# A four-branch graph network: degree reciprocals spread by DMA instead of by matmuls, zero stores issued in two row stages, and each chunk's mean taken ahead of the edge shares

## The chip, the cores and the metric

One core of a Trainium2 chip runs the program. The metric is the device time of one execution in microseconds (us), here the median of three. Engine names are those of the profile: PE (TensorE; PEld is its weight load), DVE (VectorE), ACT (ScalarE), POOL (GpSimd), SP (SyncE, which here only issues DMAs).

## The reference

The graph has 6250 nodes of 128 features and 106,250 edges, sorted by destination. Four blocks follow each other, each with a residual and a layernorm over a node's features:

```
x = layernorm(x + L0(x))   # three rounds: (h + sum of h[src] over edges into dst) @ W1, batchnorm, relu, @ W2
x = layernorm(x + L1(x))   # row, col = src, dst: agg = segment_sum(x[col], row) / max(deg, 1); relu(agg @ W1.T + b1) @ W2.T + b2
x = layernorm(x + L2(x))   # agg = segment_sum(x[src], dst) / max(deg, 1); h = agg @ W_l.T + b_l + x @ W_r.T; batchnorm, relu, + x
x = layernorm(x + L3(x))   # edge-weighted segment max, then edge-weighted mean, weights normalised per destination
```

Two vectors of degrees matter here: `deg` over the sources for L1 and `deg` over the destinations for L2. Their reciprocals scale whole columns of a `[features, nodes]` array, so every one of the 128 partitions needs the same 6250 numbers.

## The kernel before

The nodes are cut into 10 chunks (`NBLK`) of 625 columns (`BLK`), each of five tiles of 125 (`TN`). A message sum is done as a dense product: a matrix of edge counts stands in DRAM (`counts`, and transposed in `turned`), in panels of 0.8 MB, ten panels (`NSUB`) to a chunk. SP loads the panels into four buffers (`PAN`), and PE multiplies each with the node rows, which are split into three bf16 parts (`XP`, `HH`): 30 matmuls to a panel (line 524), 300 to a chunk. `pe_dense` runs such a pass; passes 1 and 2 serve L0, pass 3 (with `scales=True`) serves L1 and reads `turned`, pass 4 serves L2. Between passes lie the batchnorms and "row stages", in which PE, ACT and DVE pass single chunks back and forth (`act_unit_rows` before pass 3, `act_mean_rows` before pass 4). The row steps of a stage are woven into the first chunk of the next pass (`steps_between`): six steps stand before its first panel, one before each further one.

Where the order comes from: each engine's list is written out by hand, and engines meet only at counting semaphores. An engine works strictly through its own list, and so does a DMA queue's issuer: a DMA that ACT issues stands between ACT's other instructions.

What the change touches:

- **The reciprocals.** DVE computes them as 125 partitions x 50 (`rin` for L2, in `dve_in_degrees`; `rdeg` for L1, in `dve_row_sums`). To bring 625 of them onto all partitions DVE lays five of the 50 columns out as diagonal matrices (lines 994 and 1052), PE multiplies a matrix of ones with them (lines 507 and 514), and ACT copies the product out of PSUM into `DEG` (line 588) or `A` (line 1403). That happens once a chunk, ten times in pass 1 and ten times in pass 3.
- **The edge shares.** 104 groups of edges are handled beside passes 1 and 3, 52 in each (`WEIGH_AT`: seven or six groups to a chunk in pass 1, six in pass 3). For a group ACT issues two loads of 0.576 MB (`share_loads`, line 578; two buffers), DVE compares and sums them (`dve_shares`, line 845), and POOL scatters the result into the array `shares` in DRAM (line 761).
- **The zeros.** `shares` has to be zero before the scatters reach it. Half is zeroed at the start. The rest takes 25 stores of 3.2 MB from a zero array in DRAM (`blank_slices`, line 565): five after pass 1, one a chunk in pass 2, and ten together at the start of `act_unit_rows`.
- **The mean in pass 3.** `dve_mean` takes chunk c's six groups of shares first and then multiplies chunk c's sums with its reciprocals (line 1062). PE's linear layer of that chunk (line 488) needs this product. It stands before panel 3 of chunk c + 1.

Of the kernel before, what the change touches and what calls it, by code (L numbers as in the profile page):

```python
# [41 lines left out]
ZEROS_AT = {"dense1": (0,) * 10, "taken1": 5, "dense2": (1,) * 10, "taken2": 10}  # L42
# [5 lines left out]
def build_program(nc, a, out):  # L48
# [3 lines left out]
    with ctx:  # L52
# [14 lines left out]
        blank = nc.dram_tensor("blank", [128, 6400], F32).ap()  # L67
        share_rows = nc.dram_tensor("share_rows", [1, EP + 256], F32).ap()
# [114 lines left out]
        in_mat = [AA[0:TN, 5000 + b * BLK:5000 + (b + 1) * BLK].rearrange("p (j n) -> p j n", n=TN) for b in range(2)]  # L183
# [4 lines left out]
        scale_mat = [SS[b][0:TN, :].rearrange("p (j n) -> p j n", n=TN) for b in range(2)]  # L188
# [25 lines left out]
        degree_ps = [PS[:, 2048 + 512 * h:2048 + 512 * h + n] for h, n in ((0, HALF), (1, BLK - HALF))]  # L214
# [48 lines left out]
        in_diag = sem("in_diag")  # L263
        in_full = sem("in_full")
        in_kept = sem("in_kept")
        scale_diag = sem("scale_diag")
        scale_full = sem("scale_full")
        scale_kept = sem("scale_kept")
# [209 lines left out]
        def pe_dense(pe, n, lin, terms, ready, taken=None, degrees=False, scales=False, own=True, between=None):  # L478
# [13 lines left out]
            for c in range(NBLK):  # L492
# [5 lines left out]
                for s in range(NSUB):  # L498
# [3 lines left out]
                    if degrees and s == (1 if c else NSUB - 1):  # L502
                        pe.wait_ge(in_diag, c + 1)
                        pe.wait_ge(in_kept, c + 2)
                        for h, (lo, w) in enumerate(((0, HALF), (HALF, BLK - HALF))):
                            last = nc.tensor.matmul(degree_ps[h], ones[0:TN, :],
                                                    AA[0:TN, 5000 + b * BLK + lo:5000 + b * BLK + lo + w],
                                                    start=True, stop=True)
                        last.then_inc(in_full, 1)
                    if scales and s == (1 if c else NSUB - 1):  # L510
                        pe.wait_ge(scale_diag, c + 1)
                        pe.wait_ge(scale_kept, c + 2)
                        for h, (lo, w) in enumerate(((0, HALF), (HALF, BLK - HALF))):
                            last = nc.tensor.matmul(degree_ps[h], ones[0:TN, :], SS[b][0:TN, lo:lo + w],
                                                    start=True, stop=True)
                        last.then_inc(scale_full, 1)
# [67 lines left out]
        def keep_degrees(act, c):  # L584

            act.wait_ge(in_full, c + 1)
            for h, (lo, w) in enumerate(((0, HALF), (HALF, BLK - HALF))):
                last = nc.scalar.activation(DEG[:, c * BLK + lo:c * BLK + lo + w], degree_ps[h], ACT.Copy)
            last.then_inc(in_kept, 1)

        def act_dense(act, n):

            for c in range(NBLK):
                if n == 1:
                    keep_degrees(act, c)
# [3 lines left out]
                if n == 1 and c == 0:  # L599
                    act.wait_ge(xp_ready, 2 * NBLK)  # L600
# [389 lines left out]
        def dve_in_degrees(dve):  # L990

            def spread(c):
# [10 lines left out]
            dve.drain()  # L1003
            nc.vector.reciprocal(rin[0:TN, :], rin[0:TN, :])
            dve.drain()
            spread(0)
            spread(1)
            dve_unit_weights(dve)
            dve.wait_ge(unit_rows, 1)
# [1586 lines left out]
```

## Time and profile before

| | us |
|---|---|
| median of three runs | 4531.61 (4524.09 to 4542.86) |
| profiled execution, its own time | 4542.64 |
| span of its profile | 4540.8 |
| granted TensorE clock, mean of the span | 0.930 |

The span falls into the build of the matrices with pass 0 (to about 1240 us), pass 1 (1277 to 1736), pass 2 (1774 to 2225), the first row stage and pass 3 (2232 to 2764), the second row stage and pass 4 (2765 to 3229), the row stage of L2 (to 3300) and L3 (to the end). Durations below are from this one execution, so sums are made against its own time. A view with 40 digits cuts its window in 40 equal slices; a digit is the busy share in tenths.

### The profile page before, as it was taken

What the parts mean: (1) busy time and instruction counts of PE and PEld (TensorE: products, weight loads), DVE (VectorE), ACT (ScalarE), POOL (GpSimd) and SP (SyncE); (2) the same over time, 40 slices, a digit from 0 to 9 for tenths busy, and PEclk for the clock granted to TensorE, in tenths of its full rate; (3) what the DMA queues carried; (4) which work ended last, traced back from release to release, by engine and by line L of the source; (5) the groups of instructions that cost most, each with busy time, mean ns of one, the idle gap of its engine ahead of it and who ended that gap; (6) DMA issues with size and microseconds to landing.
All of it is one profiled execution on the core that took longest, in us unless ns stands there. A gap on an engine that the chain in (4) does not pass through costs nothing.

```text
span 4540.8 us, 71772 instructions
## 1 busy us (share of the span) xinstructions
PE 3528.8 (78%) x24919; PEld 2671.7 (59%) x24919; DVE 2066.2 (46%) x5903; ACT 1059.9 (23%) x2743; POOL 2450.1 (54%) x2510
## 2 busy tenths in 40 slices
PE   0005987555589998899769998999847898989898
PEld 0004766444466665677546776777546777777776
DVE  6543434443254556877655544000333444444445
ACT  0003655333420002000130003000323333333331
POOL 4777777777203444444305443444267777777750
PEclk9999998777799999999889999999868999999999
DMA  9999999887449998788899993666244777767665
GB/s 373 368 363 360 368 368 336 291 282 266 165 151 334 351 360 279 262 282 278 282 341 331 360 340 123 189 196 195 86 128 159 243 261 246 259 236 261 237 232 188
DMA packets 307375, 1218.26 MB, mean 268 GB/s; under 512 B 86273, under 2 KB 98850, under 8 KB 290811
## 3 DMA queue, kind: packets, MB, share of 16 engines
q1 hardware_dynamic: 143706, 705.58, 43.9%
q10 hardware_dynamic: 83489, 453.14, 27.0%
q0 software_dynamic: 79872, 55.32, 5.2%
q8 instruction: 207, 3.39, 0.3%
q14 instruction: 101, 0.83, 0.1%
HBM read 958.19 MB, written 337.54 MB: 285 GB/s over the span
## 4 chain that ended last, share of the span: by engine, by line
PE 42%; POOL 23%; DMA 16%; issue 10%; DVE 4%; ACT 2%; POOLq 1%; ACTq 1%; DVEq 0%; SPq 0%
PE PS L524 30%; POOL PAN L389 18%; DMA counts<-SSB 8%; POOL counts L735 5%; PE PS L446 4%; DMA BB<-share_rows 4%; DMA counts<-val_slot,idx_slot 2%; PE PS L1462 2%; PE PS L452 1%; DMA PAN<-counts 1%; PE PS L488 1%; DVE ST L845 1%; DMA PAN<-turned 1%; DVE X L882 1%; PE PS L1112 1%
## 5 line engine op out<-in xcount | busy, mean ns | idle before, releaser
L761 POOL DMA_INDIRECT shares<-dst_f,spare x832 | 810.2, 974 | 1247.6 <-DMA shares<-dst_f,spare 468.7
L524 PE MATMUL PS<-PAN,HH 125*128 125x375 bf16 x8000 | 1413.3, 299 | 36.8 <-DMA PAN<-turned 12.1
L389 POOL DMA_INDIRECT PAN<-table,src_i x832 | 820.0, 986 | 347.8 <-issue 273.1
L735 POOL DMA_INDIRECT counts<-val_slot,idx_slot x832 | 807.1, 970 | 350.0 <-issue 323.0
L524 PEld LDWEIGHTS PS<-PAN,HH 125*128 125x128 bf16 x8000 | 780.8, 98 | 340.2 <-issue 34.0
L524 PE MATMUL PS<-PAN,XP 125*128 125x375 bf16 (+1 forms) x4000 | 866.3, 298 | 0.0
L446 PE MATMUL PS<-PAN,HH 125*128 125x375 bf16 x2000 | 363.7, 305 | 608.9 <-DMA PAN<-counts 608.9
L446 PEld LDWEIGHTS PS<-PAN,HH 125*128 125x128 bf16 x2000 | 180.4, 101 | 650.6 <-issue 485.4
L524 PEld LDWEIGHTS PS<-PAN,XP 125*128 125x128 bf16 x4000 | 390.5, 98 | 153.0 <-issue 3.7
L656 ACT ACTIVATE X<-PS 125x625 bf16<-125x625 bf16 x500 | 345.2, 692 | 453.2 <-PE PS L452 441.6
L882 DVE TENSOR_REDUCE X<-PAN 125x5 f32<-125x3125 bf16 x100 | 334.2, 3399 | 76.0 <-DMA PAN<-counts 76.0
L1548 ACT ACTIVATE BB<-PAN,ew 128x128 f32<-128x128 f32 x832 | 254.2, 388 | 476.4 <-DMA PAN<-table,src_i 476.4
L845 DVE SCALAR_TENSOR_TENSOR BB<-BB 128x255 bf16<-128x255 f32 x312 | 135.3, 485 | 392.4 <-DMA BB<-share_rows 392.1
L1462 PE MATMUL PS<-XP,HH 125*128 125x375 f32 (+1 forms) x1000 | 287.3, 436 | 13.0 <-DVE HH L1654 13.0
L1462 PE MATMUL PS<-PAN,HH 125*128 125x375 f32 (+1 forms) x1000 | 288.3, 437 | 1.8 <-issue 1.8
L907 DVE SCALAR_TENSOR_TENSOR ST<-BB,spare 128x255 bf16<-128x255 f32 x624 | 262.5, 484 | 35.7 <-DMA BB<-key_rows 18.3
L928 DVE CAST val_slot<-acc 128x8 bf16<-128x8 f32 x104 | 21.9, 211 | 562.1 <-DMA counts<-val_slot,idx_slot 561.7
L1614 DVE TENSOR_TENSOR_SCAN BB<-BB,PS 128x1024 f32<-128x1024 f32 x104 | 243.4, 2340 | 15.3 <-PE PS L1430 15.3
L452 PEld LDWEIGHTS PS<-ident_h,PAN 125*125 125x125 bf16 x2500 | 213.8, 141 | 51.2 <-ACT X L656 19.2
L452 PE MATMUL PS<-ident_h,PAN 125*125 125x125 bf16 x2500 | 230.7, 224 | 11.5 <-ACT X L656 11.3
L1641 DVE TENSOR_TENSOR DEG<-DEG,PS 128x375 f32<-128x375 f32 (+1 forms) x180 | 85.7, 480 | 330.8 <-PE PS L1462 330.8
L1462 PEld LDWEIGHTS PS<-XP,HH 125*128 125x128 f32 x1000 | 187.1, 195 | 77.7 <-DVE HH L1654 14.7
(271 smaller groups left out, 3937.7 us busy)
## 6 DMA issues: line engine op xcount, KB each, us to landing
PAN<-counts SPq DMA_DIRECT2D x300, 800.0 KB
counts<-SSB ACTq DMA_DIRECT2D x10, 8000.0 KB, 35.8
shares<-SSB SPq DMA_DIRECT2D x50, 1600.0 KB
PAN<-counts ACTq DMA_DIRECT2D x100, 800.0 KB
shares<-blank ACTq DMA_DIRECT2D x25, 3200.0 KB, 22.9
XP<-shares SPq DMA_DIRECT2D x50, 1600.0 KB
PAN<-shares SPq DMA_DIRECT2D x50, 1600.0 KB
turned<-X ACTq DMA_DIRECT2D x100, 781.2 KB
```

Of the source, the lines that this page charges most:

```text
L389: nc.gpsimd.indirect_dma_start(out=gbuf[g % 2][:, k, :], out_offset=None, in_=source, in_offset=bass.IndirectOffsetOnAxis(ap=src_i[:, t:t ...
L446: nc.tensor.matmul(dense_ps[b][h], xpart[part][0:TN, s * SUBJ + j, :], panel[u % NPAN][0:TN, j, lo:lo + w], start=(s == 0 and j == 0 and p ...
L452: last = nc.tensor.transpose(turn_ps[m][0:TN, k, 0:TN], panel[u % NPAN][0:TN, k, j * TN:(j + 1) * TN], ident_h[0:TN, 0:TN])
L524: last = nc.tensor.matmul(dense_ps[b][h], xpart[part][0:TN, s * SUBJ + j, :], (turned_tile if scales else panel)[u % NPAN][0:TN, j, lo:lo ...
L656: nc.scalar.activation(stage[u % NTURN][0:TN, t, :, :], turn_ps[m][0:TN, :, 0:TN], ACT.Copy, accum_out=in_sums[:, s, bass.ds(i * (2 * TPB) ...
L735: nc.gpsimd.indirect_dma_start(out=counts_flat, out_offset=bass.IndirectOffsetOnAxis(ap=idx_slot[b][:, k:k + 1], axis=0), in_=val_slot[b][ ...
L761: nc.gpsimd.indirect_dma_start(out=shares_flat, out_offset=bass.IndirectOffsetOnAxis(ap=share_at[:, t:t + 1], axis=0), in_=share[:, t:t + ...
L882: nc.vector.tensor_reduce(out=sums[:, c, p * SUBJ:(p + 1) * SUBJ], in_=panel[u % NPAN][0:TN, :, 0:BLK], axis=AX.X, op=ALU.add).then_inc(pa ...
L907: last = nc.vector.scalar_tensor_tensor(out=junk[k], in0=KR[b][:, k * 128:k * 128 + NEAR], scalar=key_e[:, at(k, 1)], in1=mask[:, :], op0= ...
L1462: last = nc.tensor.matmul(part_ps[h], h_rows[0:TN, c * SUBJ + j, :], wpanel[u % NWP][0:TN, j, lo:lo + w], start=(j == 0), stop=(j == SUBJ ...
L1548: last = nc.scalar.activation(weighed[:, k, :], gbuf[g % 2][:, k, :], ACT.Copy, scale=ew[:, g * GT + k:g * GT + k + 1])
L1614: nc.vector.tensor_tensor_scan(scan[g % 2], pen[g % 2], msg_ps, scan[1 - g % 2][:, GE - 1:GE], ALU.add, ALU.max).then_inc(scanned, 1)
```

## The change

The reciprocals go through a small DRAM array, `degree_rows`. `store_degrees` writes the 125 x 50 array into it in the order of the nodes (`(j p) -> p j`, so that neighbours in a partition lie 500 bytes apart in DRAM, and every 4-byte number is a run by itself). `spread_degrees` reads the row of 6250 numbers back onto all 128 partitions (a 3.2 MB load). Both are issued by ACT. The diagonals, the matmuls with ones and the copies out of PSUM are gone. The ten zero stores at the start of `act_unit_rows` are gone from there; one now follows each of five steps of that row stage and of the next. In `dve_mean` a chunk's product stands before its shares, and in `act_scales` four of a chunk's six share loads stand behind the next linear output.

```diff
-        def keep_degrees(act, c):
-            act.wait_ge(in_full, c + 1)
-            for h, (lo, w) in enumerate(((0, HALF), (HALF, BLK - HALF))):
-                last = nc.scalar.activation(DEG[:, c * BLK + lo:c * BLK + lo + w], degree_ps[h], ACT.Copy)
-            last.then_inc(in_kept, 1)
+        def store_degrees(act, which, rows, ready, out_sem):
+            act.wait_ge(ready, 1)
+            act.dma_start(degree_rows[which:which + 1, :].rearrange("o (j p) -> p (o j)", p=TN), rows[0:TN, :],
+                          allow_slow_non_contiguous=True
+                          ).then_inc(out_sem, 16)
+        def spread_degrees(act, which, to, out_sem, spread_sem):
+            row = degree_rows[which:which + 1, :]
+            act.wait_ge(out_sem, 16)
+            act.dma_start(to, bass.AP(row.tensor, row.offset, [[0, 128], [1, N]])).then_inc(spread_sem, 16)
...
         def act_dense(act, n):
             for c in range(NBLK):
-                if n == 1:
-                    keep_degrees(act, c)
                 if c:
                     act_linear_chunk(act, 2 * n, c - 1, ACT.Identity, f"L0_b1_{n}", A)
                 keep_dense(act, n, c // 2, c % 2)
                 if n == 1 and c == 0:
+                    store_degrees(act, 0, rin, rin_ready, rin_out)
...
                 if n == 1:
                     if c == 1:
                         act.wait_ge(share_rows_out, 16 * 3)
+                    if c == 3:
+                        spread_degrees(act, 0, DEG[:, 0:N], rin_out, rin_spread)
                     share_loads(act, WEIGH_AT[1][c])
...
         def dve_mean(dve):
-            scale(0, 0)
-            scale(0, 1)
             dve.wait_ge(xp_ready, 4 * NBLK)
             share_keys(dve)
             for c in range(NBLK):
+                if c == 0:
+                    dve.wait_ge(rdeg_spread, 16)
+                mean(c // 2, c % 2)
                 dve_shares(dve, WEIGH_AT[3][c])
-                mean(c // 2, c % 2)
-                if c + 2 < NBLK:
-                    scale(c // 2 + 1, c % 2)
...
             act.wait_ge(bn_coef, 5)                      # act_unit_rows
             for c in range(2):
                 act_affine_chunk(act, A, c)
-            blank_slices(act, ZEROS_AT["taken2"], known=False)
+            store_degrees(act, 1, rdeg, rdeg_ready, rdeg_out)
             for k in range(NBLK + 3):
...
+                blank_slices(act, int(1 < k < 7), known=False)
...
         def act_mean_rows(act):
...
+                blank_slices(act, int(k < 7), known=False)
...
         def act_scales(act):
+            spread_degrees(act, 1, A[:, 0:N], rdeg_out, rdeg_spread)
             act.wait_ge(xp_ready, 4 * NBLK)
             for c in range(NBLK):
-                act.wait_ge(scale_full, c + 1)
-                for h, (lo, w) in enumerate(((0, HALF), (HALF, BLK - HALF))):
-                    last = nc.scalar.activation(A[:, c * BLK + lo:c * BLK + lo + w], degree_ps[h], ACT.Copy)
-                last.then_inc(scale_kept, 1)
                 if c == 3:
                     blank_slices(act, 0)
-                share_loads(act, WEIGH_AT[3][c] // 2)
                 if c:
                     act_linear_chunk(act, 6, c - 1, ACT.Relu, "L1_b1", A)
-                share_loads(act, WEIGH_AT[3][c] - WEIGH_AT[3][c] // 2)
+                    share_loads(act, WEIGH_AT[3][c - 1] - min(WEIGH_AT[3][c - 1], 2))
+                share_loads(act, min(WEIGH_AT[3][c], 2))
```

`pe_dense` loses the two blocks that issued the matmuls with ones. `act_linear_chunk` of pass 4 now confirms the last zeros to POOL at chunk 3. Both arrays of reciprocals are stored and spread once.

How the lists read, first ACT's at the start of the first row stage. L1223 (L1192 after) is the affine step, L565 (L548) a zero store, L570 the new store of reciprocals. Before:

```order
606 L1894 ACTIVATE cf<-mv,eps_bn 128x1
607 L1223 ACTIVATE AA<-AA,cf 128x625 x2
608 L565 DMA shares<-blank 128x6400 x10
609 L1223 ACTIVATE AA<-AA,cf 128x625 x2
610 L1231 ACTIVATE SSB,col_slot<-PS 125x128 x5
```

The same place after the change:

```order
588 L1862 ACTIVATE cf<-mv,eps_bn 128x1
589 L1192 ACTIVATE AA<-AA,cf 128x625 x2
590 L570 DMA degree_rows<-rdeg 125x50x1
591 L1192 ACTIVATE AA<-AA,cf 128x625 x2
592 L1200 ACTIVATE SSB,col_slot<-PS 125x128 x5
...
598 L1178 ACTIVATE ST<-ST,row_mv,row_sd 125x128 x5
599 L1183 ACTIVATE HH<-ST 125x640
600 L548 DMA shares<-blank 128x6400
601 L1192 ACTIVATE AA<-AA,cf 128x625
```

One store of 125 x 50 single numbers has taken the place of ten zero stores, and the first zero store has moved behind the first normalized chunk.

DVE's list at the start of pass 3, where L845 (L835 after) are the shares and L1062 (L1032) is the mean. Before:

```order
733 L1052 TENSOR_TENSOR SSB<-ident,rdeg 125x625 x2
734 L833 SCALAR_TENSOR_TENSOR BB<-keyloc,src_i 128x832
735 L845 SCALAR_TENSOR_TENSOR BB,dst_f<-BB 128x255 x3
736 L845 SCALAR_TENSOR_TENSOR ST,dst_f<-BB 128x255 x5
...
746 L845 SCALAR_TENSOR_TENSOR ST,dst_f<-BB 128x255 x5
747 L1062 TENSOR_TENSOR AA<-AA,PS 128x375
748 L1062 TENSOR_TENSOR AA<-AA,PS 128x250
749 L1052 TENSOR_TENSOR SSB<-ident,rdeg 125x625
```

After:

```order
724 L823 SCALAR_TENSOR_TENSOR BB<-keyloc,src_i 128x832
725 L1032 TENSOR_TENSOR AA<-AA,PS 128x375
726 L1032 TENSOR_TENSOR AA<-AA,PS 128x250
727 L835 SCALAR_TENSOR_TENSOR BB,dst_f<-BB 128x255 x3
728 L835 SCALAR_TENSOR_TENSOR ST,dst_f<-BB 128x255 x5
```

The mean of chunk 0 has moved ahead of the first six groups, and the diagonals (L1052) are gone.

ACT's list where pass 3 begins. L1403 is the copy out of PSUM, L578 (L561 after) a share load, L546 (L529) the output of the linear layer, L578 after the change the spread. Before:

```order
675 L1219 ACTIVATE X<-PS 128x625
676 L1403 ACTIVATE AA<-PS 128x375
677 L1403 ACTIVATE AA<-PS 128x250
678 L578 DMA BB<-key_rows 128x1151
679 L578 DMA BB<-share_rows 128x1151
```

After:

```order
662 L1188 ACTIVATE X<-PS 128x625
663 L578 DMA AA<-degree_rows 128x6250
664 L561 DMA BB<-key_rows 128x1151
665 L561 DMA BB<-share_rows 128x1151
666 L561 DMA BB<-key_rows 128x1151
667 L561 DMA BB<-share_rows 128x1151
668 L529 ACTIVATE AA<-PS,vectors 128x625
669 L561 DMA BB<-key_rows 128x1151
```

The first linear output now stands behind two groups' loads, where nine stood ahead of it before.

## Rows read from the trace of the kernel before

**Rows 1.** Busy by stretch: PE, PEld, DVE, ACT, POOL, PEclk, DMA share, GB/s. Pass 1.
```profile
1371.00:1420.00 49.00, 47.23 (x353) 33.87 (x351) 22.59 (x109) 2.89 (x7) 17.69 (x19) 1.00 1.00 373
```
**Rows 2.** The same view, the two row stages.
```profile
2225.00:2345.00 120.00, 75.17 (x390) 50.41 (x391) 67.98 (x240) 61.65 (x203) 0.00 (x0) 0.77 1.00 351
2764.00:2835.00 71.00, 58.00 (x356) 40.94 (x357) 44.80 (x159) 34.81 (x81) 16.69 (x17) 0.95 0.27 83
```
**Rows 3.** Timeline of ACT, passes 1 and 2: start, us, instruction [idle before <-releaser].
```profile
1327.68 0.48 ACT L552 ACTIVATE AA<-PS 128x375 f32<-128x375 f32 x1 [4.10 <-PE PS L473]
1370.96 0.48 ACT L552 ACTIVATE AA<-PS 128x375 f32<-128x375 f32 x1 [26.23 <-PE PS L473]
...
1735.98 0.75 ACT L552 ACTIVATE AA<-PS 128x375 f32<-128x375 f32 x2 [17.40 <-PE PS L473]
...
2182.22 0.48 ACT L552 ACTIVATE AA<-PS 128x375 f32<-128x375 f32 x1 [28.28 <-PE PS L473]
2224.45 0.48 ACT L552 ACTIVATE AA<-PS 128x375 f32<-128x375 f32 x1 [28.28 <-PE PS L473]
```
**Rows 4.** Waits of PE from 1270 to 1740 us: total, times, longest.
```profile
PE PS L506 <- DVE AA L994: 11.6, 4, 3.9
```
**Rows 5.** DMA from 1371 to 1736 us: all; one queue (packets, MB, share).
```profile
DMA packets 32000, 127.37 MB, mean 349 GB/s; under 512 B 8416, under 2 KB 8416, under 8 KB 31968
...
q0 software_dynamic: 5472, 0.10, 1.1%
```
**Rows 6.** Timeline of ACT, start of the first row stage.
```profile
2231.37 17.67 ACTq L565 DMA_DIRECT2D shares<-blank  x8
2249.09 1.71 ACT L1223 ACTIVATE AA<-AA,cf 128x625 f32<-128x625 f32 x2 [17.20 <-issue]
...
2259.59 0.74 ACT L1214 ACTIVATE HH<-ST 125x640 bf16<-125x640 f32 x1
```
**Rows 7.** Chain that ended last, 2215 to 2400 us: start, us, what.
```profile
2276.10 4.18 PE PS L524 x30
...
2309.67 33.81 DMA PAN<-turned
...
2349.90 1.07 PE PS L514 x4
```
**Rows 8.** Line 524 of PE, whole span: idle before it until, us, times.
```profile
  DMA PAN<-turned: 12.1, 3
```
**Rows 9.** Timeline of PE, first linear layer of pass 3.
```profile
2392.40 2.47 PE L488 MATMUL PS<-AA,weights 128*128 128x512 f32 x4 [24.25 <-DVE AA L1062]
```
**Rows 10.** Chain that ended last, second row stage.
```profile
2791.49 4.03 PE PS L524 x30
...
2834.93 24.20 PE PS L524 x180
2859.13 2.15 PE PS L488 x8
```
**Rows 11.** Chain that ended last, inside pass 3.
```profile
2480.28 32.27 PE PS L524 x240
...
2522.75 32.27 PE PS L524 x240
```
**Rows 12.** DMA issues: KB each, median us from issue to landing.
```profile
BB<-in_x_rows ACTq DMA_DIRECT2D x1, 3200.0 KB, 24.9
```
**Rows 13.** Line 1741: SP issues ten stores of 125 partitions, duration ns min/median/max.
```profile
L1741 SPq DMA_DIRECT2D out<-BB x10: 264/2712/5948, 4499.9 to 4534.5; - x10
```
**Rows 14.** DMA from 4503 to 4541 us: share in 40 slices; the queue.
```profile
DMA  9923433333333333333333343333333100233300
...
q1 hardware_dynamic: 6380, 4.02, 34.2%
```
**Rows 15.** Timeline of POOL in pass 2, two scatters of 128 numbers.
```profile
2203.09 0.96 POOL L761 DMA_INDIRECT shares<-dst_f,spare  x1 [0.30 <-issue]
2204.35 0.95 POOL L761 DMA_INDIRECT shares<-dst_f,spare  x1 [0.30 <-issue]
```

More of the change, by code:

```diff
@@ L182, in build_program @@
         in_sums = DEG[0:TN, 5728:5728 + NBLK * NBLK * TPB].rearrange("p (c j) -> p c j", c=NBLK)
-        in_mat = [AA[0:TN, 5000 + b * BLK:5000 + (b + 1) * BLK].rearrange("p (j n) -> p j n", n=TN) for b in range(2)]
         near_w, near_k, same, before, behind = (BB[0:G, j * KRW:(j + 1) * KRW] for j in range(5))
@@ L187, in build_program @@
         sums = X[0:TN, 0:NBLK * NBLK * TPB].rearrange("p (c j) -> p c j", c=NBLK)
-        scale_mat = [SS[b][0:TN, :].rearrange("p (j n) -> p j n", n=TN) for b in range(2)]
         KR = [BB[:, b * KRW:b * KRW + KRS] for b in range(2)]
@@ L262, in build_program @@
         turned_out = [sem(f"turned_out{u}") for u in range(NTURN)]
[L263 to L268, printed above, removed]
+        rin_ready = sem("rin_ready")
+        rin_out = sem("rin_out")
+        rin_spread = sem("rin_spread")
+        rdeg_ready = sem("rdeg_ready")
+        rdeg_out = sem("rdeg_out")
+        rdeg_spread = sem("rdeg_spread")
         near_in = sem("near_in")
@@ L476, in add_own, with pe_dense @@
             return last
-        def pe_dense(pe, n, lin, terms, ready, taken=None, degrees=False, scales=False, own=True, between=None):
+        def pe_dense(pe, n, lin, terms, ready, taken=None, scales=False, own=True, between=None):
             taken = (dense_taken, NBLK * n + 1) if taken is None else taken
@@ L501, in pe_dense @@
                         between(s)
-                    if degrees and s == (1 if c else NSUB - 1):
-                        pe.wait_ge(in_diag, c + 1)
-                        pe.wait_ge(in_kept, c + 2)
-                        for h, (lo, w) in enumerate(((0, HALF), (HALF, BLK - HALF))):
[L506 to L512, printed above, removed]
-                        for h, (lo, w) in enumerate(((0, HALF), (HALF, BLK - HALF))):
-                            last = nc.tensor.matmul(degree_ps[h], ones[0:TN, :], SS[b][0:TN, lo:lo + w],
-                                                    start=True, stop=True)
-                        last.then_inc(scale_full, 1)
                     if s == 3 and c:
@@ L990, in dve_in_degrees @@
         def dve_in_degrees(dve):
-            def spread(c):
-                dve.wait_ge(in_kept, c + 1)
-                nc.vector.tensor_tensor(
-                    out=in_mat[c % 2], in0=ident[0:TN, 0:TN].unsqueeze(1).to_broadcast([TN, TPB, TN]),
-                    in1=rin[0:TN, c * TPB:(c + 1) * TPB].unsqueeze(2).to_broadcast([TN, TPB, TN]),
-                    op=ALU.mult).then_inc(in_diag, 1)
             dve.wait_ge(turn_taken, NBLK * NSUB * TPB + 4)
@@ L1003, in dve_in_degrees @@
             dve.drain()
[L1004 to L1007, printed above, removed]
+            nc.vector.reciprocal(rin[0:TN, :], rin[0:TN, :]).then_inc(rin_ready, 1)
             dve_unit_weights(dve)
@@ L1012, in dve_in_degrees @@
                 dve_shares(dve, WEIGH_AT[1][c])
-                if c + 2 < NBLK:
-                    spread(c + 2)
                 if c == NBLK // 2:
@@ L2275, in usual_rest @@
                 for c in range(NBLK):
+                    if c == 3:
+                        blank_slices(act, 0)
                     act_linear_chunk(act, 8, c, ACT.Identity, "L2_b_l", B)
@@ L2480, in usual_rest @@
                 pe_linear(pe, 1, [("L0_W2_0", A)], after_src=(aff_done, 0))
-                pe_dense(pe, 1, 2, [("L0_W1_1", A)], (dense_taken, NBLK + 2), degrees=True, between=rows_between(pe, 0))
+                pe_dense(pe, 1, 2, [("L0_W1_1", A)], (dense_taken, NBLK + 2), between=rows_between(pe, 0))
                 pe_units(pe)
```

19 lines of the change are left out of this document (5 added, 14 removed).

## The prediction

> **What bounds the kernel now.** I read the chain of waits first, in the stretch that the change touches (1277 to 3229 us), then the waits of PE and the timeline of ACT, and last the DMA queues. In these four passes PE is the bound: inside pass 3 two chunks follow each other at 42.47 us [rows 11], in pass 2 at 42.23 [rows 3], and nothing stands between their matmuls. What is to be gained lies at three places.
>
> First, pass 1. Chunks 0 to 1 are 43.28 us apart, 1.05 us more than in pass 2, and from there to the last chunk 408.3 us go by where nine such steps are 389.5 [rows 3]. The 18.8 us over are stalls: PE waited 11.6 us in four stalls for DVE's diagonals [rows 4], which stand behind a chunk's seven groups, and the rest is lower clock and knock-on after them. The DMA engines have little left there: 349 GB/s on average [rows 5], 373 GB/s where their share is 1.00 [rows 1].
>
> Second, the start of the first row stage. ACT issues ten zero stores, its queue backs up, and its next operation starts after 17.20 us of idle time [rows 6]. Everything in that stage hangs on this operation. The stores then hold the DMA engines at a share of 1.00 and 351 GB/s for 120 us [rows 2], and PE waits for panels of `turned`, 12.1 us in three waits [rows 8], one of which the chain of waits gives as a transfer of 33.81 us [rows 7].
>
> Third, the first mean of pass 3. Chunk 0 ends at 2349.90 + 1.07 + 4.03 = 2355.0 (line 514 stands before its last panel) [rows 7, 10]. PE does three panels of chunk 1 and one more product with ones, and stops 24.25 us, till 2392.4 [rows 9], because DVE takes six groups of shares before the mean.
>
> **The change part by part.**
>
> *The matmuls with ones go.* One set costs 1.07 us of PE [rows 7], or 1.05 by the pitch. Pass 1: 10 x 1.05 = 10.5. With them goes the wait for the diagonals: 18.8. Together 29.3, if the DMA engines follow. They carry 127.37 MB in the 365 us from 1371 on [rows 5], and the spread of `rin` adds 3.2. At the full-share rate of 373 that is 350 us, at an unchanged 349 it is 374. So that stretch can give 15 us, or lose 9; the first two chunks give 2 more. I take 17, since a stretch with seven groups already runs at that rate with PE 96% busy [rows 1]. DVE's 10 diagonals and ACT's 20 copies lay in idle time of their engines: nothing.
>
> *The ten zero stores go from the start of the row stage.* 17.2 us less one issue of 0.6: 16.6.
>
> *The first chunk of pass 3.* From its first panel to its end it takes 78.9 us (2276.10 to 2355.0) [rows 7]. The same weave in the second row stage, where the DMA share is 0.27 [rows 2], takes 55.5: 2791.49 to 2859.13 less three panels of 4.03 [rows 10]. Gain 23.4. The five zero stores that remain are 16 MB, about 46 us at 351 GB/s, and start behind chunk 0's first step; the four panels in the buffers and PE's slow pace there should cover them.
>
> *The mean goes ahead.* From the end of chunk 0 to the linear layer 37.4 us pass (2355.0 to 2392.4), and three panels need 12.1. Gain 25.3. Later in the pass nothing changes: four loads start after linear output c, some 14 us into chunk c + 1, and the mean has 12 us of grace behind the chunk's end.
>
> *What is late next* is the spread. ACT issues it when the last row step is through, 43 us after the first panel, and a load of its size landed in 24.9 us [rows 12]. So it lands at 68, and PE wants the product at 55.5 + 12.1 = 67.6. I take 2 us of wait.
>
> *Rest of pass 3:* 8 sets of 1.05 are 8.4, and the first linear layer no longer runs at half clock (2.47 us [rows 9], where two such sets take 2.15 [rows 10]): 1.2. *Second row stage:* five zero stores between ACT's steps, at a DMA share of 0.27 [rows 2]: from 0 to -10, I take -3 for both row stages.
>
> *The store of the reciprocals* is the unknown. Each of the 6250 numbers is a run of 4 bytes. The nearest rows are SP's last stores: also 125 partitions, also to DRAM, 625 runs of 512 bytes each. They use 0.3 of the DMA engines, flat, so 5 of 16, at 34.2% x 16 x 38 us / 6380 = 33 ns a run with all else in it [rows 14], and at their steady 108 GB/s 24 ns a run and engine. And they hold their issuer: one issue takes 2.7 us (median), 5.9 at most [rows 13]. With x ns a run and 5 engines our store lasts D = 1.25x us, and ACT cannot issue its next DMA until it is nearly through.
> In the row stage the store starts to move at about 2234 (pass 2's last zero store, issued at 2224.45 [rows 3], needs 9 us before it), and ACT reaches its first zero store 11.2 us after the stage's start (2249.09 to 2260.3 [rows 6]), at 2244. The stall is S = D - 9. In pass 1 it starts at 1328.5, and PE misses ACT only at the third panel of chunk 2, 1383: loss P = D - 54.
> Bounds for x: POOL's scatters of single numbers give 1.1% x 16 x 365 us / 5472 = 12 ns a packet, and a packet there is 128 x 171 / 5472 = 4 numbers: 3 ns [rows 5]. From above, POOL sends 128 numbers over 16 engines every 1.26 us: not over 158 ns [rows 15]. I take 24, the row of the same kind. Then D = 30, S = 21, P = 0.
>
> A rule speaks against this store. The Trainium skill, page "DMA: Bandwidth & Descriptors", section "Rules for kernel authors", says that a strided last dimension becomes one descriptor per element and should be made contiguous. The stores' 6380 packets for ten times 625 runs agree. The same page, section "Why a DMA increments its semaphore by 16 and not by 1", has the number of engines as the largest divisor up to 16 of the outer dimension, 5 for 125; the flat 0.3 agrees. On 16 engines D would be 9 us, S = 0, and the sum 21 us better.
>
> **Sum.** 17 + 16.6 + 23.4 + 25.3 - 2 + 9.6 - 3 = 87, less S = 21: a gain of 66 us. The profiled execution took 4542.64 (span 4540.8 and 1.8 around it), so 4476.6; the median of the runs lies 11.0 below it, so I forecast 4531.6 - 66 = 4466.
>
> **The rivals.**
>
> *A. The small runs are cheap.* At x = 10 D is 12.5 and S 3.5: gain 83, 4448. For it: 3 ns a number in the scatters [rows 5], and of the 24 ns of a 512-byte run some 22 are the bytes themselves, at 373 / 16 GB/s an engine [rows 1]. Against: those are packed by POOL, and HBM writes of 4 bytes have no row on this queue. This chance is nearly as large as the forecast's.
>
> *B. Small writes cost double.* If a run is read, merged and written back it takes about twice a 512-byte one, x = 48: D = 60, S = 51, P = 6, gain 30, 4502. Nothing in the trace shows it. The skill's page on DMA has such a rule in its opening table: below 512 bytes the engine does a read-modify-write.
>
> *C. Slower.* The store holds ACT's queue so long that ACT, in its order, cannot do the row steps behind the first zero store, and in pass 1 not the copy of chunk 1. With 87 gained, S + P = 2D - 63 turns the sign at D = 75, that is x = 60. At x = 85, D = 106: gain 87 - 149 = -62, 4594. For it: ACT stood still for 17.2 us behind ten plain stores [rows 6], SP up to 5.9 us behind 625 runs [rows 13]; here there are ten times as many. Against: 60 ns is 2.5 times the nearest row.
>
> *D. Pass 1 gives nothing.* DMA holds its 349 GB/s [rows 5]; then -7 stands for 17: gain 42, 4490.
>
> **How the numbers follow.** Forecast 0.32, A 0.30, B 0.13, C 0.13, D 0.12. From no change a measurement of this kernel can tell about 0.5%, 23 us. Faster by more: forecast, A, most of B and D: 0.80. Within: rest of B and the near side of C: 0.07. Slower: 0.13. The range reaches from 4435 (A with pass 1's full 29) to 4535, just past the break-even of C. The forecast's own range is 4452 to 4482.
>
> **What would show it.** ACT's timeline behind the new store in the row stage: idle before the first zero store 21 us (forecast), under 5 (A), over 50 (B, C). Landing of the store of reciprocals: 30 us. PE's line 524 with under 4 us of waits for `turned`. The wait of the first linear layer in pass 3: under 5 us from 24.25, with its releaser the spread. Pitch in pass 1 from 45.4 to about 43.4, in pass 3 from 42.47 to 41.4. DMA in pass 1 above 365 GB/s. I am wrong if the stall behind the store exceeds 70 us, if PE waits for panels in the second row stage, or if pass 1 keeps its pitch.

## The result, and the profile after

| | before | after |
|---|---|---|
| median of four runs | 4530.79 us (4524.09 to 4542.86) | 4465.48 us (4455.56 to 4466.75) |
| profiled execution | 4542.64 | 4465.78 |
| span, granted clock | 4540.8, 0.930 | 4464.1, 0.930 |

The ratio is 0.9848, with a 95% interval of 0.9823 to 0.9873: 65 us faster, where 66 were forecast. The two profiled executions are 76.9 us apart, since the one of before lay 11.9 above its median.

To see where the time went, both traces are cut at marks that exist in both: ACT's first copy of a kept chunk (line 535, before 552), PE's first dense matmul of a pass (507, before 524) and ACT's linear outputs (529, before 546).

| stage | before | after | gain | forecast |
|---|---|---|---|---|
| A: start to chunk 0 of pass 1 kept | 1327.7 | 1323.4 | 4.3 | 0 |
| B: chunks 1 to 9 of pass 1 | 408.3 | 391.0 | 17.3 | 17 |
| C: to the first panel of pass 2 | 38.1 | 42.7 | -4.6 | 0 |
| D: pass 2, to its last kept chunk | 450.4 | 449.4 | 1.0 | 0 |
| E: first row stage, to the first panel of pass 3 | 51.4 | 42.1 | 9.3 | 16.6 - 21 |
| F: to the first linear output of pass 3 | 121.3 | 73.9 | 47.4 | 46.7 |
| G: to the last linear output of pass 3 | 368.5 | 361.8 | 6.7 | 9.6 |
| H: to the first linear output of pass 4 | 95.6 | 104.8 | -9.2 | -3 (E to H) |
| I: to the last linear output of pass 4 | 371.5 | 371.5 | 0 | 0 |
| J: row stage of L2 and L3 | 1307.9 | 1303.4 | 4.5 | 0 |

The 1.2 us that the forecast gave for the first linear layer at full clock are counted under G there, though by these marks they fall into F.

The total was met, but not by its terms. Timeline of ACT at the start of the first row stage, after; columns as in [rows 3], to be held against [rows 6]:

```profile
2206.53 0.50 ACTq L548 DMA_DIRECT2D shares<-blank  x1
...
2212.27 0.28 ACTq L570 DMA_DIRECT2D degree_rows<-rdeg  x1
2213.08 2.49 ACT L1192 ACTIVATE AA<-AA,cf 128x625 f32<-128x625 f32 x3
2220.57 0.28 ACT L1200 ACTIVATE SSB<-PS 125x128 bf16<-125x128 f32 x1 [5.00 <-PE PS L1088]
...
2229.35 3.56 ACTq L548 DMA_DIRECT2D shares<-blank  x1
2232.95 0.91 ACT L1192 ACTIVATE AA<-AA,cf 128x625 f32<-128x625 f32 x1 [2.88 <-issue]
```

The 17.20 us of idle time before L1192 are gone. The new store is issued in 0.28 us, and the first DMA behind it holds ACT for only 2.88 us, where 21 were forecast. The DMA view of two stretches behind it shows why, all packets of each:

```profile
DMA packets 3388, 0.03 MB, mean 4 GB/s; under 512 B 3387, under 2 KB 3387, under 8 KB 3387
...
DMA packets 547, 0.21 MB, mean 103 GB/s; under 512 B 539, under 2 KB 539, under 8 KB 539
```

The first row is 2222 to 2230 us: 423 small writes a microsecond. On the five engines of the forecast that is one in 11.8 ns each; the view doesn't count engines, and its packets take 58.8% of 16 engines' time, 22 ns each, so they overlap or more engines work. The second row is 2232 to 2234, in which the store runs out. It has the queue from 2219.2, when the zero store ahead of it is through, to 2233.2, so D is 14.0 us, not 30.

The chain that ended last, from there to pass 3 (against [rows 7]), and its later part (against [rows 10, 11]):

```profile
2248.83 4.05 PE PS L507 x30
...
2300.75 12.31 DMA PAN<-turned
...
2321.42 1.07 PE PS L486 x4
...
2612.34 40.33 PE PS L507 x300
2652.67 1.07 PE PS L486 x4
...
2730.06 25.27 DMA PAN<-counts
...
2762.73 24.20 PE PS L507 x180
2786.93 2.15 PE PS L486 x8
```

The transfer of 33.81 us is now 12.31, the linear layer L486 starts at full clock (1.07) with no wait before it, and a chunk of pass 3 takes 41.40. But a new transfer of 25.27 us stands in the second row stage, where the DMA share was 0.27 at 83 GB/s [rows 2]. With zero stores in that stage the share is 0.77, at 262 GB/s:

```profile
2684.00:2787.00 103.00, 86.04 (x534) 60.40 (x533) 47.39 (x162) 35.57 (x81) 48.27 (x50) 0.90 0.77 262
```
PE's waits for panels, 2212 to 2325 us, against [rows 8]:

```profile
PE PS L507 <- DMA PAN<-turned: 0.5, 1, 0.5
```

Pass 1, ACT's timeline against [rows 3]:

```profile
1323.69 23.36 ACTq L589 DMA_DIRECT2D ST<-in_bias_rows  x1
...
1348.11 0.78 ACT L529 ACTIVATE AA<-PS,vectors 128x625 f32<-128x625 f32 x1 [23.99 <-issue]
...
1450.05 0.33 ACTq L578 DMA_DIRECT2D DEG<-degree_rows  x1
...
1503.59 0.78 ACT L529 ACTIVATE AA<-PS,vectors 128x625 f32<-128x625 f32 x1 [52.80 <-DVE ST L835]
```

Here the bias load behind the store held ACT for 23.36 us, which PE did not feel: the first three steps are 42.23 each. Then the spread of 3.2 MB goes out at 1450, ACT waits for share buffers, and the step over it is 54.2 us long. The stretch 1366 to 1714 in the DMA view (against [rows 5]) and the chain at its end:

```profile
DMA packets 31390, 130.12 MB, mean 374 GB/s; under 512 B 7817, under 2 KB 7817, under 8 KB 31231
```

```profile
1713.19 5.67 DMA BB<-share_rows
...
1720.18 2.12 DVE ST L835 x10
...
1722.40 0.63 ACTq L548
```

DMA runs at 374 GB/s throughout: it is the bound of pass 1. PE ends at 1714, but the last share loads land at 1718.9 and ACT goes on at 1722.4, 8 us behind its last kept chunk, where it took 2.3 before.

### The profile page after: what moved, and what is told of

It reads as the page before. It is cut to its first block, busy times and chain, and to the rows that moved or that the text cites. A ratio compares the mean times of both kernels' runs of the same rounds, so it can differ in the third digit from the quotient of the medians.

```text
span 4464.1 us, 71523 instructions
## 1 busy us (share of the span) xinstructions
PE 3506.4 (79%) x24839; PEld 2663.0 (60%) x24839; DVE 2050.4 (46%) x5883; ACT 1045.6 (23%) x2703; POOL 2442.1 (55%) x2510
## 4 chain that ended last, share of the span: by engine, by line
PE 36%; POOL 26%; DMA 17%; issue 12%; DVE 5%; POOLq 1%; ACT 1%; another core or an unknown queue 1%; ACTq 1%; DVEq 0%; SPq 0%
PE PS L507 28%; POOL PAN L387 18%; POOL counts L725 7%; DMA counts<-SSB 7%; DMA BB<-share_rows 6%; DMA counts<-val_slot,idx_slot 2%; PE PS L444 2%; PE PS L1430 2%; DMA PAN<-counts 1%; DVE ST L835 1%; PE PS L486 1%; DVE BB L835 1%; PE PS L450 1%; POOLq L719 1%
## 5 line engine op out<-in xcount | busy, mean ns | idle before, releaser
L646 ACT ACTIVATE X<-PS 125x625 bf16<-125x625 bf16 x500 | 345.1, 692 | 450.1 <-PE PS L450 433.0
L835 DVE SCALAR_TENSOR_TENSOR BB<-BB 128x255 bf16<-128x255 f32 x312 | 135.2, 484 | 372.7 <-DMA BB<-share_rows 372.7
```

What stands on the lines that cost most here:

```text
L646: nc.scalar.activation(stage[u % NTURN][0:TN, t, :, :], turn_ps[m][0:TN, :, 0:TN], ACT.Copy, accum_out=in_sums[:, s, bass.ds(i * (2 * TPB) ...
```

## The experiments

The stages of every kernel (A and J vary by 14 and 18 us on the chips of the other runs, with next to nothing changed in them). The first four ran on another chip, on which A and J took some 25% longer for every kernel (before took 5254.75 us there). B did not, nor G but for one step of e4; D was 10 to 17 us longer in all four, and I in two. So these four are read by their stages, and small differences in them say little.

| | A | B | C | D | E | F | G | H | I | J |
|---|---|---|---|---|---|---|---|---|---|---|
| e1 long runs | 1673.1 | 389.7 | 43.6 | 460.5 | 38.9 | 74.7 | 361.8 | 103.1 | 376.7 | 1637 |
| e2 two stores | 1683.2 | 394.2 | 43.3 | 466.0 | 56.3 | 74.4 | 361.8 | 100.9 | 389.3 | 1650 |
| e3 ten together | 1661.3 | 389.5 | 44.2 | 459.1 | 61.6 | 100.1 | 362.0 | 127.5 | 371.5 | 1639 |
| e4 mean behind | 1680.2 | 386.1 | 45.2 | 461.4 | 41.7 | 106.5 | 385.7 | 102.6 | 371.5 | 1620 |
| e5 spread in pass 2 | 1319.4 | 380.0 | 46.3 | 455.0 | 42.7 | 73.6 | 361.8 | 104.1 | 371.5 | 1306 |
| e6 zeros in pass 4 | 1321.3 | 394.9 | 44.1 | 449.1 | 42.2 | 75.7 | 361.8 | 99.2 | 372.2 | 1303 |
| e8 both moved | 1314.1 | 380.0 | 43.5 | 456.4 | 41.5 | 73.2 | 361.8 | 98.0 | 371.5 | 1306 |
| e7 ones kept | 1325.1 | 402.4 | 37.7 | 450.1 | 38.8 | 76.3 | 370.3 | 104.1 | 371.5 | 1318 |
| e9 mean alone | 1322.7 | 397.1 | 37.2 | 451.2 | 53.7 | 95.1 | 370.3 | 97.5 | 371.5 | 1301 |
| e11 zeros alone | 1324.2 | 399.8 | 36.9 | 451.4 | 39.8 | 102.7 | 369.3 | 103.5 | 371.5 | 1300 |
| e12 sixteen engines | 1319.9 | 400.7 | 43.5 | 450.3 | 43.5 | 73.3 | 361.8 | 102.8 | 371.5 | 1308 |
| e10 pieces | 1316.9 | 389.5 | 44.8 | 450.2 | 44.1 | 73.2 | 361.8 | 95.8 | 371.8 | 1300 |

The theory after the traces: the store costs little; mean and zeros make E and F; pass 1 is bound by DMA; the moved zeros cost H. The rivals stand in each expectation.

**e1, the store in long runs.**

```diff
-"o (j p) -> p (o j)"
+"o (p j) -> p (o j)"
```

> The store of reciprocals writes each partition's 50 numbers as one run of 200 bytes (125 runs instead of 6250), so the numbers come out in another order; nothing else is changed. Theory (the store costs only the stall of its issuer): ACT's idle time of 2.9 us behind the first zero store of the row stage falls below 0.5, the 24 us of idle time in pass 1 behind the bias load fall below 6, and the time falls by 3 us to about 4462. Rival (6250 writes of 4 bytes also slow the zero stores and panels beside them): the stretch from the start of the first row stage to the first linear layer of pass 3 (109.2 us) shortens by 8 or more, and the time is 4457 or less.

The reciprocals reach the wrong nodes in it, so it serves for times alone. 5160.62 us, ratio to before 0.9844 (0.9795 to 0.9894), too wide for 3 us. ACT's timeline, the same place:

```profile
2572.67 0.28 ACTq L570 DMA_DIRECT2D degree_rows<-rdeg  x1
...
2589.52 0.51 ACTq L548 DMA_DIRECT2D shares<-blank  x1
```

The zero store takes 0.51 us instead of 3.56, and E is 38.9 instead of 42.1: the store costs 3.2 us there. In pass 1 the bias load issues in 0.31 us instead of 23.36, but ACT's idle time falls only to 18.28 us where under 6 was expected: it now waits for DVE. So behind the hold of 24 us stood a wait of 18 that was there anyway. B does not change beyond its scatter (386 to 395 in four kernels that share its code there). E and F together gain 2.4 us, where the rival asked for 8 or more: it falls.

**e2, the store twice.**

```diff
-            act.dma_start(degree_rows[which:which + 1, :] ...
+            for to in (which, which + 2):
+                act.dma_start(degree_rows[to:to + 1, :] ...
```

> Each store of reciprocals is issued twice in a row, the second into rows that nobody reads. Theory (the queue takes one store's runs one after another on 5 engines, about 20.6 to 23.4 us each, and ACT cannot issue past them): ACT is held in pass 1 for 44 to 47 us instead of 24, still under the 54 after which PE would miss it, so pass 1 loses nothing. In the row stage the stall before the first zero store grows from 2.9 to about 24 us, all of it on PE's path: the time is 4486, up 21. Rival (ACT is not held by the store's length, the 2.9 us come from the zero stores around it): stall under 6 us and a time within 4 us of 4465.

5198.84 us, 0.9905 (0.9874 to 0.9936). ACT's timeline, pass 1 and row stage:

```profile
1683.22 22.72 ACTq L571 DMA_DIRECT2D degree_rows<-rin  x2
...
1705.98 20.45 ACTq L590 DMA_DIRECT2D ST<-in_bias_rows  x1
...
1728.06 0.78 ACT L529 ACTIVATE AA<-PS,vectors 128x625 f32<-128x625 f32 x1 [44.09 <-issue]
...
2592.50 20.11 ACTq L571 DMA_DIRECT2D degree_rows<-rdeg  x2
```

The holds add up: a second store issues only when the first is nearly through (22.72), the next DMA waits for the second (20.45). In the row stage the hold is 20.11 us and then 3.50 behind the next DMA. E grows by 14.2, not 21: idle time behind DMAs goes from 2.88 to 18.45 + 3.50 us, but ACT's 5.00 us of waiting for PE shrink to 0.45, since PE works on during the hold. Pass 1: the first step took 45.5 instead of 42.2, and no row shows PE waiting for it.

**e3, ten zero stores together again.**

```diff
+            blank_slices(act, 10, known=False)
             store_degrees(act, 1, rdeg, rdeg_ready, rdeg_out)
-                blank_slices(act, int(1 < k < 7), known=False)
-                blank_slices(act, int(k < 7), known=False)
```

> All ten zero stores stand at the start of the first row stage again, the store of reciprocals behind them, and none between the row steps of either stage. Theory: ACT stalls there for 17 us as before the change, chunk 0 of pass 3 takes some 79 us from its first panel instead of 60.5 to the product (PE waits for turned 12 us instead of 0.5), and the second row stage gets back the 9.2 us that it lost: +17 +18 -9 = +26, about 4491. Rival 1 (the ten stores were hidden; only the mean gained): within 5 us of 4465. Rival 2 (the store of reciprocals behind the ten comes too late, after 91 us of zeros, and the spread with it): the wait of the first linear layer of pass 3 is over 10 us and the time is 4505 or more.

5232.64 us, 0.9974 (0.9940 to 1.0008): hardly faster than before. ACT, then PE at the first linear layer of pass 3:

```profile
2561.14 19.05 ACTq L548 DMA_DIRECT2D shares<-blank  x8
2580.24 8.64 ACTq L570 DMA_DIRECT2D degree_rows<-rdeg  x1
2588.92 1.71 ACT L1192 ACTIVATE AA<-AA,cf 128x625 f32<-128x625 f32 x2 [27.31 <-issue]
...
2701.56 0.33 ACTq L578 DMA_DIRECT2D AA<-degree_rows  x1
```

```profile
2713.28 2.48 PE L486 MATMUL PS<-AA,weights 128*128 128x512 f32 x4 [15.36 <-DVE AA L1032]
```

The second rival holds: behind ten zero stores the reciprocals reach DRAM late, the spread starts at 2701.56, and PE waits 15.36 us for the mean. E and F lose 45.7 us, where 35 were expected. So with the store behind the zeros in ACT's queue the DMA way loses what it won; it needs the zeros out of its way. H is no evidence: it holds a gap of 24.2 us in which neither PE nor ACT does anything and DMA is nearly idle, which I cannot explain.

**e4, the mean behind the shares again.**

```diff
-                mean(c // 2, c % 2)
                 dve_shares(dve, WEIGH_AT[3][c])
+                mean(c // 2, c % 2)
```

> DVE takes a chunk's six groups of shares before the mean again, and ACT's share loads stand in the order of before. Theory: the first linear layer of pass 3 waits about 25 us for DVE, as before the change; the rest of pass 3 keeps its 41.4 us a chunk: time 4490. Rival (with fewer zero stores in flight the share loads come faster, a group in 6.6 us instead of 11, so the order costs little): a wait under 12 us, time 4476 or less.

5215.44 us, 0.9936 (0.9902 to 0.9970). Waits of PE (total, times, longest):

```profile
PE PS L486 <- DVE AA L1032: 28.3, 1, 28.3
```

28.3 us, and F is 32.6 longer: the order makes the wait, with the zeros gone as well. The rest of pass 3 keeps 41.4 a chunk but for one of 65.4, in which matmuls stand about 1 us apart with no releaser; not explained, and seen nowhere else.

**e5, the first spread in pass 2.**

```diff
+                if n == 2 and c == 5:
+                    spread_degrees(act, 0, DEG[:, 0:N], rin_out, rin_spread)
...
-                    if c == 3:
-                        spread_degrees(act, 0, DEG[:, 0:N], rin_out, rin_spread)
```

> The spread of the in-degrees' reciprocals (3.2 MB) is issued in pass 2, before chunk 5, instead of in pass 1; nothing else is changed. Theory (pass 1 is bound by the DMA engines, at 374 GB/s): from the end of chunk 0 of pass 1 to the first panel of pass 2 the kernel after takes 433.7 us (391.0 and 42.7); 3.2 MB less are 8.6 us less, 425, the step of 54.2 us from chunk 3 to 4 falls below 47, pass 2 keeps 42.23 a chunk: time 4457 where the kernel after has 4465.5. Rival (pass 1 is bound by ACT and DVE passing the two share buffers to and fro, not by bytes): these two stages stay above 430 and the time above 4462.

4457.33 us (4449.23 to 4462.17), 0.9837 (0.9824 to 0.9851). Pass 1 by stretch, columns as in [rows 1]:

```profile
1361.70:1699.50 337.80, 337.74 (x2552) 244.13 (x2550) 175.20 (x818) 12.27 (x25) 149.15 (x151) 1.00 1.00 373
```

PE is busy in 337.74 of 337.80 us and B is at its floor of nine times 42.23. B and C together fall from 433.7 to 426.3, the bytes' worth less 1.2, with DMA still at 373: the theory of pass 1 holds. Pass 2, which should have lost nothing, loses 5.6, in one step of 47.2: the spread followed directly behind a zero store, 6.4 MB ahead of the panels. So stages B to I give only 2 us; the other 6 of the median can't be placed.

**e6, the second row stage's zeros in pass 4.**

```diff
-                blank_slices(act, int(k < 7), known=False)
...
-                    if c == 3:
+                    if c < 5:
+                        blank_slices(act, 1, known=False)
+                    if c == 5:
                         blank_slices(act, 0)
```

> The five zero stores between the row steps of the second row stage stand in pass 4 instead, one ahead of each of its first five linear outputs, and are confirmed at chunk 5. Theory (they cost the second row stage 9.2 us, since the panels of counts queue behind 16 MB, while in pass 4 the DMA share is 0.59): from the last linear output of pass 3 to the first of pass 4 it takes 95.6 us as before the change instead of 104.8, pass 4 keeps 42.49 us a chunk, time 4456. Rival 1 (the 9 us are not the zeros'): still above 102. Rival 2 (POOL's scatters now wait for the zeros and end after pass 4): the end of the program moves back by what is won.

4459.61 us (4453.28 to 4465.43), 0.9844 (0.9831 to 0.9857). H falls from 104.8 to 99.2. With the zeros in that stage H is 101 to 105 in eight kernels (e3 has none there), without them 95.6 to 99.2 in five: they cost 6 to 7 us rather than 9.2. I goes up by 0.7, J does not. In this trace B came out 3.9 longer with the same pass 1, so stages B to I together gain nothing; the 6 us are read from H over all kernels.

**e8, both.**

> Both moves together: the spread of the in-degrees' reciprocals in pass 2 and the second row stage's five zero stores in pass 4. The two stages do not touch each other, so the gains should add: 8.6 and 9.2 make 18, time 4448. Rival (one of them only moves a wait): 4456 or more.

4453.09 us (4444.97 to 4461.01), 0.9833 (0.9818 to 0.9848): 12 below the kernel after, where 18 were expected, with 8 and 6 for the parts. Both moves show in B and H, pass 2 pays 7 us in D, and stages B to I together give 11.

**e7, the matmuls with ones kept; e9 and e11, one edit each on the kernel before.**

```diff
 # e9 (and e7)
+                mean(c // 2, c % 2)
+                if c + 2 < NBLK:
+                    scale(c // 2 + 1, c % 2)
                 dve_shares(dve, WEIGH_AT[3][c])
-                mean(c // 2, c % 2)
 # e11 (and e7), at the start of act_unit_rows
-            blank_slices(act, ZEROS_AT["taken2"], known=False)
+                blank_slices(act, int(1 < k < 7), known=False)
```

> The kernel before with two of the three edits: zero stores spread over the row stages, and each mean (with the linear output's share loads) ahead of the shares. The reciprocals still come from diagonals, matmuls with ones and copies. Theory (what the DMA way is worth by itself): pass 1 as before, 408 us instead of 391 (+17), its end 38 instead of 43 (-5), the row stage without the store's stall 39 instead of 42 (-3), pass 3 371 instead of 362 (+9), first chunk +1: time 21 above the kernel after, 4486. Rival (the DMA way's gain comes back elsewhere): within 8 us of it.

> The kernel before with one edit: in pass 3 the mean stands ahead of the chunk's shares (diagonals behind it) and the share loads behind the linear output. Ten zero stores, matmuls with ones and all else as before. Theory (the 24.25 us wait of the first linear layer is made by the order alone): the wait falls below 2 us, the stretch from the first panel of pass 3 to its first linear output falls from 121.3 to 96 us, the rest of pass 3 gains nothing but stays at 42.5 a chunk: time 4506. Rival (the share loads that had the DMA engines to themselves during the wait now meet the panels, and later chunks of pass 3 pay): pass 3 from its first to its last linear output goes above 375 us (368.5 before) and the time is above 4515.

> The kernel before with one edit: the zero stores spread over the two row stages (and confirmed in pass 4 at chunk 3). Mean behind the shares, matmuls with ones as before. Theory (terms add): last kept chunk of pass 2 to first panel of pass 3 51.4 to 39, first chunk of pass 3 23 us shorter, second row stage and first chunk of pass 4 8 us longer: -28, time 4503. Rival (the zeros and the mean's order share a gain: with the order of before PE waits for DVE's six groups, whose loads end the wait whatever the panels do): the stretch from the first panel to the first linear output shortens by under 12 us, and the time is 4512 or more.

e7 took 4486.53 (4471.11 to 4495.73), 0.9901 (0.9884 to 0.9918); e9 4506.90, 0.9945 (0.9926 to 0.9965); e11 4504.92, 0.9936 (0.9915 to 0.9957). PE in e11:

```profile
2349.93 2.47 PE L488 MATMUL PS<-AA,weights 128*128 128x512 f32 x4 [23.61 <-DVE AA L1062]
```

The order alone takes the wait away: in the whole of e9 PE's linear layers (L488) wait 1.0 us for the mean. In stage F the two edits add: 26.2 for the mean, 18.6 for the zeros, 45.0 for both. In E the zeros give 11.6 to 14.9 (e9 to e7). By the medians 45 us of the gain are order, and the DMA way is worth the remaining 21, as e7's expectation had it. By stages it is 8.5 in G, 11.4 in B and 2.4 in F, less 5.0 in C and 3.3 in E, together 14; the rest can't be placed, and A and J scatter by more. Three more traces of pass 1 with the matmuls also show B at 402.4, 397.1 and 399.8, and PE's waits for the diagonals at 10.2, 6.5 and 7.7 us, so the 408.3 of the profile before was a long one. With C, which ends that pass, the four take 446.4, 440.1, 434.3 and 436.7 us; the kernel after takes 433.7, and e3, e4 and e6 with the same pass 1 433.7, 431.3 and 439.0. Pass 1 gains some 5 us from the DMA way, not 12.7.

**e12, the store on sixteen engines.**

```diff
-            act.dma_start(degree_rows[...].rearrange("o (j p) -> p (o j)", p=TN), rows[0:TN, :], ...
+            for lo, hi in ((0, 112), (112, TN)):
+                act.dma_start(degree_rows[...].rearrange("o (j p) -> p (o j)", p=TN)[lo:hi, :], rows[lo:hi, :], ...
```

> Each store of reciprocals is issued as two, of 112 partitions (a multiple of 16) and of 13; the same 6250 runs of 4 bytes to the same places. Theory (each of k engines writes its runs one after another at some 19 ns, and 125 partitions use only 5): 350 runs an engine and 50 for the rest take 7.5 us instead of 20 to 23; ACT is held in pass 1 for under 10 us instead of 24, the 2.9 us stall of the row stage goes, and from the last kept chunk of pass 2 to the first panel of pass 3 it takes 38.9 us instead of 42.1: time 4462. Rival (writes of 4 bytes have one limit in common whatever the number of engines): ACT held for 20 us or more, 42 us, time 4465.

4471.31 us (4458.64 to 4478.41), 0.9854 (0.9831 to 0.9878): no gain. ACT in the row stage, the DMA view of 2225 to 2228 us and of 2228 to 2231, and pass 1 by stretch:

```profile
2220.13 10.88 ACTq L571 DMA_DIRECT2D degree_rows<-rdeg  x2
2231.05 1.71 ACT L1192 ACTIVATE AA<-AA,cf 128x625 f32<-128x625 f32 x2 [9.22 <-issue]
```

```profile
DMA packets 3012, 0.45 MB, mean 149 GB/s; under 512 B 2995, under 2 KB 2995, under 8 KB 2995
...
DMA packets 1551, 0.01 MB, mean 2 GB/s; under 512 B 1551, under 2 KB 1551, under 8 KB 1551
```

```profile
1324.00:1331.00 7.00, 7.00 (x55) 5.05 (x53) 6.86 (x6) 0.00 (x0) 0.00 (x0) 1.00 2.11 12
```

The writes begin at about 2226.3 and end at 2235.3: 9 us for what took 14.0. By 2228, 1.7 us on, 2995 of the 6250 are under way; then come 517 a microsecond, and 450 in the three after (1351 packets), close to the 423 of the undivided store. So there is a fast start and behind it a pace that the number of engines hardly changes. Neither side is right as a whole: in pass 1 ACT's longest hold is 11.55 us, near the theory's 10 and not the rival's 20, but stage E takes 43.5, above both. The form is what costs: the second, small store must wait for room, so ACT is held at once (9.22), and in pass 1, while all queues together move 12 GB/s for 7 us, PE waits 4.2 us for a panel and the first step is 49.5 us. One undivided store on 16 engines wasn't run.

**e10, three moves.**

```diff
+                if n == 2 and c % 2:
+                    at = (c // 2) * 2 * BLK
+                    act.dma_start(DEG[:, at:at + 2 * BLK], ...).then_inc(rin_spread, 16)
```

(with the zeros of e6 and the store of e12)

> The kernel after with three moves: the in-degrees' reciprocals are spread in pass 2 in five pieces of 0.64 MB, each behind a linear output, the second row stage's five zero stores stand in pass 4, and each store of reciprocals is issued as 112 and 13 partitions. Theory: to the two moves at once (4453) it gives back the 5 us that pass 2 lost when 3.2 MB came right behind a zero store (48.4 us for one chunk instead of 42.2), and 3 us of the row stage: time 4445, pass 2 at 42.2 a chunk. Rival (pass 2 loses the same to the pieces): pass 2 from its first panel to its last kept chunk still above 454 us where the kernel after has 449.4, time above 4450.

4453.13 us (4449.39 to 4456.66), 0.9821 (0.9798 to 0.9843). The pieces work: D is 450.2 with 0.64 MB behind each second linear output, and H is 95.8, as before the change. What is missing to 4445 lies in B and E. B is 389.5 where e5 and e8 have 380.0: the first step, 47.9 us, has a wait of 4.0 for a panel beside the store on sixteen engines, as in e12; a late one of 48.2 has a wait of 4.6 for ACT, and that this too goes back to the store is not shown. E is 44.1. e8 and e10 are the fastest here; their intervals still touch that of the kernel after, and stages B to I are 11 and 6 us shorter. e10 with the single store should come to 4453.1 - 9.5 - 2.0 = 4441.6, if all that is missing is the store's; that is an estimate and wasn't run.

## Why the forecast was met

**The store of reciprocals** is the term that was most wrong. I put S at 21 with x = 24 ns, from stores with 512-byte runs. x is 11.8 ns in the idle row stage, D 14.0, and S 2.9 (3.2 by e1). That is rival A (x = 10, S 3.5). I chose against it because most of the 24 ns are the bytes; the row should have been read with the bytes taken off. Two offsets moved as well: the store starts 7.0 us after the stage's start instead of 3.8, since the zero store ahead of it takes 12.7 and not 9, and ACT reaches its first zero store at 17.8 instead of 13.8. P = 0 was right: ACT was held 24 us in pass 1, and even 44 in e2 cost 3 us at most. Rivals B and C, the dear stores, are refuted. By the Trainium skill, page "DMA: Bandwidth & Descriptors", opening table, a transfer under 512 bytes is a read-modify-write; a price of twice a 512-byte run, which I drew from it for rival B, is not what this trace shows (11.8 ns against 24). The same page, section "Why a DMA increments its semaphore by 16 and not by 1", takes the largest divisor up to 16, for 125 partitions 5; no view here counts engines, but e12's quicker start fits more of them. D with 16 engines was put at 9 us and is 9 in e12, though by a fast start and a common pace and not by 24 ns a run; the gain of 21 us that I priced with it is not there, since S was only 2.9.

**The zeros in the first row stage:** 16.6 forecast, 12.6 measured (51.4 to 38.8 in e7; 11.6 to 14.9 by other pairs). While ACT stood still, PE had done its first products for free. With the stall gone, ACT waits 5.00 us for PE. I had timed the path from the end of the stall, where this work was already done.

**First chunk and mean:** 46.7 forecast, 47.4 measured, and each part by itself: mean 26.2 (25.3), zeros 18.6 (23.4), and 2.4 come with the DMA way (e7 has 76.3). Here too the hit hides a miss: the zeros gave 5 us less, and the 2 us of wait for the spread, put down against the gain, did not come. The spreads landed in 15.2 and 15.4 us, not 24.9, so PE did not wait for them:

```profile
DMA to landing us min/median/max: 15.2/15.3/15.4
```

**Pass 1:** 17 forecast, 17.3 measured against that profile, but only 6 to 11 against the other three. The rate was right (373 taken, 374 found), which refutes rival D's reason. The place was not complete: where DMA is the bound, PE's end is not the end of the stage. ACT went on 8 us behind its last kept chunk instead of 2.3, and C gave back 4.6. With C counted, pass 1 gave 12.7 us by this pair of profiles and about 5 by all traces. The 18.8 us of stalls came from one execution, and a long one.

**Rest of pass 3:** 9.6 against 6.7; the pitch is 41.40 as forecast. **Second row stage:** -3 for both stages against -9.2 in this profile, 6 to 7 in most. I had named "PE waits for panels in the second row stage" as a sign of being wrong, and it does: 5.0 us, behind a transfer of 25.27.

Added up: 12.7 + 12.6 + 47.4 + 6.7 - 9.2 - 3.2 = 67 in the stages that the change touches, against 66. S was put 18 us too high, and what C, E, G and H lose against the forecast is 18 us as well: the number was hit because two errors cancelled, and that is luck. The other 10 us between the profiles lie in A, D and J, where nothing changed. And with pass 1 at 5 and the second row stage at 6.5, as all traces have them, the sum is nearer 62 than 67; the scatter of A and J is larger than what is then missing to the 65 between the medians.

## What to carry to other kernels

Here a run of 512 bytes took 24 ns and one of 4 bytes 11.8, both counted on five engines: take the bytes off before pricing many tiny runs by a row of larger ones, and ask whom the issuer's hold reaches, since it costs only what is not waited for anyway. When a stall is removed, time the path behind it as if nothing had been done during it. A stage bound by DMA ends with its last load and not with PE's last matmul; bytes that aren't due there belong into a pass with slack. There 3.2 MB behind a zero store cost 5.6 to 7 us (e5, e8), and five pieces apart from it 0.8 (e10). A hit in the total proves no term: compare stage by stage, and with more than one trace of the kernel before.

## What the runs showed of the hardware

- Stores of 4-byte runs from 125 partitions, issued by ACT: 423 a microsecond with nothing beside (14.0 us for 6250), 20 to 23 us beside panel loads (e2). As 112 and 13 partitions 9 us: 2995 of the writes in the first 1.7 us, then 450 to 517 a microsecond (e12).
- While the divided store was written in pass 1, all queues together moved 12 GB/s (e12, 1324 to 1331 us); with the undivided one, 1328 to 1346 us in the kernel after, 188 GB/s.
- A store of 125 x 50 numbers lets its issuer go in 0.28 us; the next DMA of that engine is what waits, 20 to 23 us when it follows at once.
- Stages A and J ran 1314 to 1328 and 1300 to 1318 us on the other chips, and 1661 to 1683 and 1620 to 1650 on that of the first four runs, while pass 3 (361.8 in three of them) did not change. What was slower stays open: a scatter of 128 numbers took POOL 973 to 995 ns on average on that chip (e1, by line) and 972 to 975 in the kernel after.
